# Two fused VectorE instructions per tile for the feed-forward norms of layer 2, and an earlier place for GpSimd's clearing of a table

## The chip, the cores and the metric

The kernel runs on one core of a Trainium2 chip, as one program with one launch. The metric is the device time of that program in microseconds. Its engines are TensorE (PE; PEld is its weight load), VectorE (DVE), ScalarE (ACT), GpSimd (POOL) and SyncE (SP, which only issues DMAs). Each works through its own queue in order and waits on semaphores where it needs another's result, or its own earlier one.

## The reference, cut to what matters

Four layers of attention, cross-attention and feed-forward, each added to x (4 sequences of 256 tokens, 128 wide). Changed is work of layer 2's feed-forward, which holds two normalisations with weight and bias:

```python
x = x + _L2_ffn_ref(_layernorm(x, axis=-1), ln1_w, ln1_b, w1, b1, ln2_w, ln2_b, w2, b2)

def _L2_ffn_ref(x, ln1_w, ln1_b, w1, b1, ln2_w, ln2_b, w2, b2):
    def layernorm(x, w, b):
        mu = jnp.mean(x, axis=-1, keepdims=True)
        var = jnp.mean(jnp.square(x - mu), axis=-1, keepdims=True)
        return (x - mu) * jax.lax.rsqrt(var + EPS) * w + b
    ...
    h = layernorm(x, ln1_w, ln1_b)          # 128 wide
    h = bitlinear(h, w1, b1)                # activations to 8 bits, weights to -1, 0, 1; 128 -> 512
    h = jax.nn.gelu(h, approximate=False)
    h = layernorm(h, ln2_w, ln2_b)          # 512 wide
    out = bitlinear(h, w2, b2)              # 512 -> 128
    return out
```

## The kernel before, in words

Tokens lie on the 128 partitions: a batch (one sequence of 256 tokens) is two tiles of 128 tokens. The program is a row of stages. Around the change two of them run into each other: `stacked_attention`, which does the attentions of layer 2 (its last batches run here), and `feedforward_attentions`, which does layer 2's feed-forward and both attentions of layer 3. Each is written out in steps, with one list for each engine of what it issues in a step. `overlapped` puts the two lists of an engine together: step s of the second stage comes behind step s + 176 (`SHIFT`) of the first. So the place of an instruction in an engine's queue is fixed by its step, and no scheduler moves it.

In the first stage each step has a score product of one head (lines 650 and 651) into one of three PSUM banks, whose maximum VectorE takes (L847) and so frees the bank; a second score product (L661, L662) behind which ScalarE takes the exponential (L831); and in groups the product with the values (L755). After a batch's 16 heads VectorE splits the maxima in bf16 parts (L852 to L858) and TensorE transposes them (L698). L866 normalises values, L702 and L714 are the output's transposes and products.

In the second stage `PLAN` gives for each piece of the feed-forward the step for each of the four batches. "in" takes the statistics of x, "twice" normalises x into XN (two L2378) and takes the statistics of that, "norm1" normalises again and applies weight and bias, "quant1" rounds to 8 bits (L2387 to L2402), f1 transposes (L2153, copied by L2519), f2 multiplies by w1 (L2157, scaled by L2523 into H), "gelu" is ScalarE's, "hidden" takes the statistics of H (512 wide), "norm2" and "affine2" normalise it and apply weight and bias, "quant2" rounds, f3 transposes (L2163, copied by L2521) and f4 multiplies by w2 (L2168, added to x by L2526 to L2530). After that the attention of layer 3 begins: L2173 transposes the normalised x, L2179 makes queries and keys, L2242 scores, L2544 their maxima.

Statistics go to `moments` (mean and variance by tile). GpSimd makes rstd from them, `deviation`: a tensor_scalar that adds eps (L2591) and a power (L2593), behind which the semaphore rstd is raised. The function `centred` waits for that and issues for each tile one tensor_scalar with two columns as scalars, mean and rstd (L2378). `own` counts an instruction and `own.settle()` waits until all counted ones are through, so an instruction between two settles can't overlap with its neighbours; the two of a pair can.

```python
PLAN = {"in": (-58, -42, -24, -9), "twice": (-54, -38, -20, -6), "norm1": (-50, -34, -16, -2), "quant1": (-49, -33, -11, -1),
        ...
        "affine2": (-23, -11, 5, 15), ...}
FROM, TO = PLAN["in"][0], jobs[-1][0] + 1
```

MTR is a table of the row maxima's bf16 parts (4096 bf16 columns, in `space`) that layer 3's second score product reads; most of its rows stay zero, so GpSimd clears it once, with `bout` behind it. The readers are SyncE's copies into it and the job "b" (L2517).

Of the kernel before, what the change touches and what calls it, by code (L numbers as in the profile page):

```python
# [11 lines left out]
ALU = mybir.AluOpType  # L12
# [3 lines left out]
B, L, D = 4, 256, 128  # L16
# [23 lines left out]
                   ln2w=(128, 512), ln2b=(128, 512)),  # L40
# [150 lines left out]
def bcast(ap, at, n):  # L191

    a = ap.unsqueeze(at)
    shape = list(a.shape)
    shape[at] = n
    return a.broadcast_to(shape)
# [1759 lines left out]
def feedforward_attentions(c, before, shift):  # L1956


    nc, PS, s = c.nc, c.PS, c.space
    n = "l23"  # L1960
    WF, WA, WX = c.W["l2_ffn"], c.W["l3_attn"], c.W["l3_xattn"]
# [33 lines left out]
    stats, moments = over(TILES * 6).rearrange("p (t i) -> p t i", t=TILES), over(TILES * 2).rearrange("p (t i) -> p t i", t=TILES)  # L1995
# [10 lines left out]
    var, rstd = ({x: sem("_%s_%s" % (y, x)) for x in ("in", "twice", "hidden", "attn", "cross", "out")} for y in ("var", "rstd"))  # L2006
# [357 lines left out]
    def vector(dve, own):  # L2364
# [10 lines left out]
        def centred(kind, b, src, dst, mom, index, done=None):  # L2375
            dve.wait_ge(rstd[kind], b + 1)
            for t in range(2):
                ins = nc.vector.tensor_scalar(dst(t), src(t), mom[:, index + t, 0:1], c.rstd[:, index + t:index + t + 1],  # L2378
                                              ALU.subtract, ALU.mult)
                if done is None:  # L2380
                    own(ins)
                else:
                    ins.then_inc(done, 1)

        def quantise(b, h, tmp, q, weight, done):
            li, st, iv = (a[:, b % 2, weight, :] for a in (lim, step_, inv))
            own(nc.vector.tensor_reduce(li, h, AX_X, ALU.max, apply_absolute_value=True))  # L2387
            own.settle()
            own(nc.vector.tensor_scalar(li, li, 1e-5, None, ALU.max))
            own.settle()  # L2390
            own(nc.vector.reciprocal(st, li))
            if (b, weight) != (0, 0):
                own(nc.vector.tensor_scalar(iv, li, 1.0 / 127, wmean[:, weight:weight + 1], ALU.mult, ALU.mult))
            own.settle()
            own(nc.vector.tensor_scalar(st, st, 127.0, None, ALU.mult))
            own.settle()
            for t in range(2):
                own(nc.vector.tensor_scalar(tmp[:, t, :], h[:, t, :], st[:, t:t + 1], 127.0, ALU.mult, ALU.min))
            own.settle()
            own(nc.vector.tensor_scalar(tmp, tmp, -128.0, MAGIC, ALU.max, ALU.add))  # L2400
            own.settle()
            nc.vector.tensor_scalar(q, tmp, MAGIC, None, ALU.subtract).then_inc(done, 1)  # L2402
# [3 lines left out]
        def feedforward(what, b):  # L2406
            h = H[:, b % 2]
            ht, hn = (lambda t: h[:, t, :]), (lambda t: h[:, t, 0:D])
            if what == "in":
                statistics("in", b, xt(b), c.stats, c.moments, tile(b))  # L2410
            elif what == "twice":
                centred("in", b, xt(b), xnt(b), c.moments, tile(b))
                statistics("twice", b, xnt(b), stats, moments, tile(b))
            elif what == "norm1":
                centred("twice", b, xnt(b), hn, moments, tile(b))
                own.settle()
                own(nc.vector.tensor_tensor(h[:, :, 0:D], h[:, :, 0:D], bcast(WF["ln1w"], 1, 2), ALU.mult))
                own.settle()
                own(nc.vector.tensor_tensor(h[:, :, 0:D], h[:, :, 0:D], bcast(WF["ln1b"], 1, 2), ALU.add))
                own.settle()  # L2420
            elif what == "quant1":
                if b >= 2:
                    dve.wait_ge(*emptied("f3", b - 2, 0))
                quantise(b, h[:, :, 0:D], T[:, :, 0:D], Q[:, b % 2, :, 0:D], 0, q_ready)
            elif what == "hidden":
                dve.wait_ge(gelu_done, 2 * b + 2)
                statistics("hidden", b, ht, stats, moments, tile(b))
            elif what == "norm2":
                centred("hidden", b, ht, ht, moments, tile(b))
                own.settle()  # L2430
                own(nc.vector.tensor_tensor(h, h, bcast(WF["ln2w"], 1, 2), ALU.mult))
                own.settle()
            elif what == "affine2":
                own(nc.vector.tensor_tensor(h, h, bcast(WF["ln2b"], 1, 2), ALU.add))
                own.settle()
            elif what == "quant2":
                quantise(b, h, T, Q[:, b % 2], 1, q2_ready)
            elif what == "attn":
                statistics("attn", b, xt(b), c.stats, c.moments, tile(b))
            elif what == "normed":  # L2440
                centred("attn", b, xt(b), xnt(b), c.moments, tile(b), xn_ready)
            else:
                own.settle()
                own(nc.vector.reciprocal(wscale, wmean))
                own(nc.vector.tensor_scalar(inv[:, 0, 0, :], lim[:, 0, 0, :], 1.0 / 127, wmean[:, 0:1], ALU.mult, ALU.mult))
                own.settle()
                for i, w in enumerate(("w1", "w2")):
                    own(nc.vector.tensor_scalar(T[:, i, :], WF[w], wscale[:, i:i + 1], 1.0, ALU.mult, ALU.min))
                own.settle()
                own(nc.vector.tensor_scalar(T, T, -1.0, MAGIC, ALU.max, ALU.add))  # L2450
                own.settle()
                for i in range(2):
                    nc.vector.tensor_scalar(WQ[:, i, :], T[:, i, :], MAGIC, None, ALU.subtract).then_inc(weights_ready, 1)
# [133 lines left out]
    def gpsimd(pool, own):  # L2587
# [38 lines left out]
        for step in range(FROM, TO):  # L2626
            yield step
            for what, b in pieces(step, "in", "twice", "hidden", "attn", "cross", "out"):
                deviation(what, b, moments if what in ("twice", "hidden") else c.moments)
            if step == FROM + 14:  # L2630
                nc.gpsimd.memset(MTR, 0.0).then_inc(fills, 1)
                nc.gpsimd.memset(bout, 0.0).then_inc(fills, 1)
            if step == -2:
                pool.wait_ge(before.pv_done, before.units // 4)
                pool.wait_ge(*before.q_saved)
                pool.wait_ge(*before.k_saved)
                nc.gpsimd.memset(VB[:, :, :, :, WIDE:WIDE + 1], 1.0).then_inc(fills, 1)
            for p in pieces(step, "products", "shift", "values", "scale"):
                if p[1] not in SHARED or p[0] != "shift":
                    cross(*p)  # L2640
# [333 lines left out]
```

## Time and profile before

| | |
|---|---|
| Median of 3 runs | 1099.58 us (1098.29 to 1102.47) |
| The profiled execution | 1095.55 us |
| its span | 1093.7 us |
| TensorE busy | 815.3 us (75%) |
| VectorE busy | 611.6 us (56%) |
| ScalarE busy | 349.3 us (32%) |
| GpSimd busy | 316.2 us (29%) |

The span is the time from the first to the last recorded instruction, and the execution's own time has what lies around it. Times in the profile count from the start of the span. A busy share is a mean over stages with different limits, so it says little of the stage in question. In a timeline's row the number in brackets is idle time of the engine ahead of the row, with what ended it. In the rows of groups, 128x512 is partitions by elements.

### The profile page before, as it was taken

What the parts mean: (1) busy time and instruction counts of PE and PEld (TensorE: products, weight loads), DVE (VectorE), ACT (ScalarE), POOL (GpSimd) and SP (SyncE); (2) the same over time, 40 slices, a digit from 0 to 9 for tenths busy, and PEclk for the clock granted to TensorE, in tenths of its full rate; (3) what the DMA queues carried; (4) which work ended last, traced back from release to release, by engine and by line L of the source; (5) the groups of instructions that cost most, each with busy time, mean ns of one, the idle gap of its engine ahead of it and who ended that gap; (6) DMA issues with size and microseconds to landing.
All of it is one profiled execution on the core that took longest, in us unless ns stands there. A gap on an engine that the chain in (4) does not pass through costs nothing. (4 is left out here: it accounts for less than half of the span.)

```text
span 1093.7 us, 15967 instructions
## 1 busy us (share of the span) xinstructions
PE 815.3 (75%) x5969; PEld 591.4 (54%) x5969; DVE 611.6 (56%) x1414; ACT 349.3 (32%) x683; POOL 316.2 (29%) x318
## 2 busy tenths in 40 slices
PE   4974797892686275688877755999999996167994
PEld 2542453581353164567645433677777686144994
DVE  2654872323669962886666787764345545843222
ACT  1110474331121111245535541444342332011331
POOL 1354200203238723332221211000053433415232
PEclk9985798896688676999989886999999998558897
DMA  9302200361000003544473000000000000005685
GB/s 370 148 2 86 70 7 1 93 189 36 20 1 1 0 1 73 111 92 85 112 203 88 3 1 1 2 1 2 1 2 1 2 1 1 0 1 184 211 285 161
DMA packets 44678, 72.44 MB, mean 66 GB/s; under 512 B 4817, under 2 KB 36737, under 8 KB 43033
## 3 DMA queue, kind: packets, MB, share of 16 engines
q1 hardware_dynamic: 38921, 65.72, 20.4%
q0 software_dynamic: 1728, 3.59, 1.0%
q10 hardware_dynamic: 3952, 2.10, 0.7%
q8 instruction: 48, 0.79, 0.3%
q14 instruction: 29, 0.24, 0.1%
HBM read 58.65 MB, written 15.89 MB: 68 GB/s over the span
## 5 line engine op out<-in xcount | busy, mean ns | idle before, releaser
L847 DVE TENSOR_REDUCE space<-PS 128x2 f32<-128x512 f32 x128 | 83.2, 686 | 40.1 <-PE PS L651 39.7
L2544 DVE TENSOR_REDUCE space<-PS 128x2 f32<-128x512 f32 x64 | 43.3, 689 | 83.0 <-PE PS L2242 82.8
L831 ACT ACTIVATE annex<-PS 128x384 f32<-128x384 f32 (+1 forms) x128 | 67.2, 544 | 57.9 <-PE PS L662 29.2
L2279 PEld LDWEIGHTS PS<-space 128*128 128x128 f32 x512 | 61.2, 191 | 16.8 <-issue 16.5
L2279 PE MATMUL PS<-space 128*128 128x65 f32 x512 | 68.6, 280 | 0.0
L2259 PE MATMUL PS<-space 64*128 64x256 f32 x256 | 67.1, 403 | 0.2 <-ACT space L2362 0.2
L1947 POOL TENSOR_TENSOR space<-space 128x1536 f32<-128x1536 f32 x16 | 54.6, 3435 | 32.7 <-ACT space L1820 26.4
L2242 PE MATMUL PS<-space 64*128 64x256 f32 x256 | 62.7, 401 | 0.1
L1170 PE MATMUL PS<-space 128*128 128x128 f32 x444 | 58.2, 287 | 4.2 <-ACT space L1239 2.3
L1305 DVE TENSOR_TENSOR space<-PS,space 128x512 f32<-128x512 f32 (+1 forms) x28 | 19.2, 687 | 74.3 <-ACT space L1232 69.2
L1170 PEld LDWEIGHTS PS<-space 128*128 128x128 f32 x444 | 54.4, 200 | 6.8 <-issue 3.8
L2591 POOL TENSOR_SCALAR var_eps<-moments 128x2 f32<-128x2 f32 x16 | 3.5, 220 | 188.1 <-DVE moments L2373 188.1
L2362 ACT ACTIVATE space<-PS 128x512 f32<-128x512 f32 x64 | 37.1, 596 | 56.3 <-PE PS L2260 56.2
L2242 PEld LDWEIGHTS PS<-space 64*128 64x128 f32 x256 | 37.8, 186 | 20.5 <-issue 14.1
L226 PE MATMUL PS<-small_tile 128*128 128x512 bf16 x40 | 17.6, 619 | 32.2 <-DVE moments L211 31.5
L831 ACT ACTIVATE space<-PS 128x512 f32<-128x512 f32 x64 | 35.7, 599 | 11.8 <-PE PS L662 10.7
L1340 POOL DMA_INDIRECT l_ffn_y<-space x22 | 21.1, 957 | 54.9 <-ACT space L1223 54.9
L2179 PE MATMUL PS<-XT,weights 128*128 128x256 f32 x128 | 34.9, 410 | 1.2 <-DVE const_tile L2519 0.7
L2606 POOL TENSOR_TENSOR weights<-CTX,annex 128x2048 f32<-128x2048 f32 x6 | 26.9, 4500 | 30.2 <-ACT CTX L2340 18.6
L2617 POOL TENSOR_TENSOR weights<-const_tile,annex 128x2048 f32<-128x2048 f32 x6 | 32.6, 5442 | 7.4 <-ACT const_tile L2354 7.4
L1789 PE MATMUL PS<-const_tile,annex 128*128 128x128 f32 x64 | 14.8, 318 | 26.4 <-DVE annex L1934 26.4
L2259 PEld LDWEIGHTS PS<-space 64*128 64x128 f32 x256 | 32.3, 186 | 2.7 <-issue 0.5
(492 smaller groups left out, 2196.3 us busy)
## 6 DMA issues: line engine op xcount, KB each, us to landing
space<-in_e_l_ffn SPq DMA_DIRECT2D x22, 768.0 KB, 4.6
space<-in_e_l_ffn SPq DMA_DIRECT2D x23, 192.0 KB, 3.0
l_ffn_sorted<-in_slots SPq DMA_DIRECT2D x2, 1584.0 KB, 25.6
space<-l_attn_scratch_k SPq DMA_DIRECT2D x8, 384.0 KB
space<-l_ffn_sorted SPq DMA_DIRECT2D x10, 264.0 KB, 4.2
weights<-in_w_l_xattn SPq DMA_DIRECT2D x1, 2504.0 KB, 15.2
weights<-in_w_l_attn SPq DMA_DIRECT2D x1, 2124.0 KB, 12.0
space<-l_xattn_scratch_q SPq DMA_DIRECT2D x4, 512.0 KB, 3.4
```

Of the source, the lines that this page charges most:

```text
L831: nc.scalar.activation(P[:, u % 8, 0:keys], PS[:, 3 + u % 2, 0:keys], ACT.Exp).then_inc(exp_done, 1)
L847: nc.vector.tensor_reduce(m[:, :, at_h], max_bank(u).rearrange("p (c k) -> p c k", c=2), AX_X, ALU.max).then_inc(max_done, 1)
L1170: last = nc.tensor.matmul(PS[:, 2 * kind + g % 2, 128 * i:128 * i + 128], weight(b, kind, chunk), x, start=True, stop=True)
L1947: nc.gpsimd.tensor_tensor(PR[:, j - 1, :, :], Q[:, t % 2, :, :], bcast(KG[:, t, j, :], 1, 16), ALU.mult).then_inc(prod, 1)
L2179: last = nc.tensor.matmul(out[:, 256 * (g % 2):256 * (g % 2) + 256], w[:, 128 * g:128 * g + 128], c.XT[:, sl], start=True, stop=True)
L2242: last = nc.tensor.matmul(PS[:, max_bank[a], 256 * qc:256 * qc + 256], q[:, 128 * qc:128 * qc + 128], kk, start=True, stop=True)
L2259: nc.tensor.matmul(out, kk[:, 128 * kc:128 * kc + 128], q, start=True, stop=False)
L2279: last = nc.tensor.matmul(out, p[:, 256 * kc + 128 * qc:256 * kc + 128 * qc + 128], VB[:, b % 2, kc, h, :], start=kc == 0, stop=kc == 1)
L2362: nc.scalar.activation(P[i % 4], PS[:, exp_bank[i], :], ACT.Exp).then_inc(exp_done, 1)
L2544: nc.vector.tensor_reduce(MX[:, b % 2, :, h], PS[:, max_bank[a], :].rearrange("p (c k) -> p c k", c=2), AX_X, ALU.max).then_inc(max_done, 1)
L2606: nc.gpsimd.tensor_tensor(PR[:, t, :].rearrange("p (h g d) -> p h g d", h=16, g=16), bcast(heads(QX, t), 2, 16), bcast(heads(KX, t), 1, 16 ...
L2617: nc.gpsimd.tensor_tensor(PR[:, t, :].rearrange("p (h d g) -> p h d g", h=16, d=8), bcast(e[:, t, :].rearrange("p (h g) -> p h g", h=16), ...
```

## The change

Two things. First, `centred` and two tensor_tensor (weight, bias) give way to two scalar_tensor_tensor for each tile: `weighted` takes (x - mean) * weight, `shifted_by` takes that times rstd, plus bias. In norm1 both follow one another; of layer 2's second norm `weighted` stands in norm2 and `shifted_by` in affine2. The wait for rstd moves from the first instruction to the second. Second, the clearing of MTR and bout is issued in step FROM + 2 = -56 instead of FROM + 14 = -44.

```diff
@@ -2382,6 +2382,18 @@
                 else:
                     ins.then_inc(done, 1)
 
+        def weighted(kind, b, src, dst, weight):
+            dve.wait_ge(var[kind], 2 * b + 2)
+            for t in range(2):
+                own(nc.vector.scalar_tensor_tensor(dst(t), src(t), moments[:, tile(b) + t, 0:1], weight, ALU.subtract, ALU.mult))
+            own.settle()
+
+        def shifted_by(kind, b, h, bias):
+            dve.wait_ge(rstd[kind], b + 1)
+            for t in range(2):
+                own(nc.vector.scalar_tensor_tensor(h(t), h(t), c.rstd[:, tile(b) + t:tile(b) + t + 1], bias, ALU.mult, ALU.add))
+            own.settle()
+
         def quantise(b, h, tmp, q, weight, done):
             li, st, iv = (a[:, b % 2, weight, :] for a in (lim, step_, inv))
             own(nc.vector.tensor_reduce(li, h, AX_X, ALU.max, apply_absolute_value=True))
@@ -2412,12 +2424,8 @@
                 centred("in", b, xt(b), xnt(b), c.moments, tile(b))
                 statistics("twice", b, xnt(b), stats, moments, tile(b))
             elif what == "norm1":
-                centred("twice", b, xnt(b), hn, moments, tile(b))
-                own.settle()
-                own(nc.vector.tensor_tensor(h[:, :, 0:D], h[:, :, 0:D], bcast(WF["ln1w"], 1, 2), ALU.mult))
-                own.settle()
-                own(nc.vector.tensor_tensor(h[:, :, 0:D], h[:, :, 0:D], bcast(WF["ln1b"], 1, 2), ALU.add))
-                own.settle()
+                weighted("twice", b, xnt(b), hn, WF["ln1w"])
+                shifted_by("twice", b, hn, WF["ln1b"])
             elif what == "quant1":
                 if b >= 2:
                     dve.wait_ge(*emptied("f3", b - 2, 0))
@@ -2426,13 +2434,9 @@
                 dve.wait_ge(gelu_done, 2 * b + 2)
                 statistics("hidden", b, ht, stats, moments, tile(b))
             elif what == "norm2":
-                centred("hidden", b, ht, ht, moments, tile(b))
-                own.settle()
-                own(nc.vector.tensor_tensor(h, h, bcast(WF["ln2w"], 1, 2), ALU.mult))
-                own.settle()
+                weighted("hidden", b, ht, ht, WF["ln2w"])
             elif what == "affine2":
-                own(nc.vector.tensor_tensor(h, h, bcast(WF["ln2b"], 1, 2), ALU.add))
-                own.settle()
+                shifted_by("hidden", b, ht, WF["ln2b"])
             elif what == "quant2":
                 quantise(b, h, T, Q[:, b % 2], 1, q2_ready)
             elif what == "attn":
@@ -2627,7 +2631,7 @@
             yield step
             for what, b in pieces(step, "in", "twice", "hidden", "attn", "cross", "out"):
                 deviation(what, b, moments if what in ("twice", "hidden") else c.moments)
-            if step == FROM + 14:
+            if step == FROM + 2:
                 nc.gpsimd.memset(MTR, 0.0).then_inc(fills, 1)
                 nc.gpsimd.memset(bout, 0.0).then_inc(fills, 1)
             if step == -2:
```

VectorE's queue at norm1 of batch 0, before: the two tensor_scalar of "twice", its statistics, four maxima, norm1, a maximum and the head of quant1 (`weights` is where H, T and moments lie).

```order
L2378 TENSOR_SCALAR XN<-X,moments,rstd 128x128 x2
L2370 BN_STATS weights<-XN 128x6 x2
L2373 BN_AGGR weights<-weights 128x2 x2
L847 TENSOR_REDUCE space<-PS 128x2 x4
L2378 TENSOR_SCALAR weights<-XN,weights,rstd 128x128 x2
L2417 TENSOR_TENSOR weights<-weights 128x2x128
L2419 TENSOR_TENSOR weights<-weights 128x2x128
L847 TENSOR_REDUCE space<-PS 128x2
L2387 TENSOR_REDUCE weights<-weights 128x2
```

The same place in the changed kernel:

```order
L2378 TENSOR_SCALAR XN<-X,moments,rstd 128x128 x2
L2370 BN_STATS weights<-XN 128x6 x2
L2373 BN_AGGR weights<-weights 128x2 x2
L847 TENSOR_REDUCE space<-PS 128x2 x4
L2388 SCALAR_TENSOR_TENSOR weights<-XN,weights 128x128 x2
L2394 SCALAR_TENSOR_TENSOR weights<-weights,rstd 128x128 x2
L847 TENSOR_REDUCE space<-PS 128x2
L2399 TENSOR_REDUCE weights<-weights 128x2
```

Four instructions in place of four, all of one tile each now, and nothing around them has moved (L2399 is L2387 under its new number).

VectorE's queue at norm2 and affine2 of batch 0, before:

```order
L2519 COPY const_tile<-PS 128x256
L2378 TENSOR_SCALAR weights<-weights,rstd 128x512 x2
L2431 TENSOR_TENSOR weights<-weights 128x1024
L2370 BN_STATS stats<-X 128x6 x2
L2373 BN_AGGR moments<-stats 128x2 x2
L864 RECIPROCAL space<-PS 128x16
L866 TENSOR_TENSOR annex<-PS,space 128x2x64
L2523 SCALAR_TENSOR_TENSOR weights<-PS,weights 128x512 x2
L2434 TENSOR_TENSOR weights<-weights 128x1024
```

and in the changed kernel:

```order
L2523 COPY const_tile<-PS 128x256
L2388 SCALAR_TENSOR_TENSOR weights<-weights 128x512 x2
L2370 BN_STATS stats<-X 128x6 x2
L2373 BN_AGGR moments<-stats 128x2 x2
L864 RECIPROCAL space<-PS 128x16
L866 TENSOR_TENSOR annex<-PS,space 128x2x64
L2527 SCALAR_TENSOR_TENSOR weights<-PS,weights 128x512 x2
L2394 SCALAR_TENSOR_TENSOR weights<-weights,rstd 128x512 x2
```

Three instructions became two at norm2, and one became two at affine2; the line numbers of the copy and of f2's scaling are four higher.

GpSimd's queue where the second stage begins, before:

```order
L2591 TENSOR_SCALAR var_eps<-moments 128x2
L2593 TENSOR_TENSOR rstd<-var_eps,neghalf 128x2
L2591 TENSOR_SCALAR var_eps<-weights 128x2
L2593 TENSOR_TENSOR rstd<-var_eps,neghalf 128x2
L2631 MEMSET space 128x4096
L2632 MEMSET space 128x128
L2591 TENSOR_SCALAR var_eps<-moments 128x2
```

and in the changed kernel:

```order
L2595 TENSOR_SCALAR var_eps<-moments 128x2
L2597 TENSOR_TENSOR rstd<-var_eps,neghalf 128x2
L2635 MEMSET space 128x4096
L2636 MEMSET space 128x128
L2595 TENSOR_SCALAR var_eps<-weights 128x2
L2597 TENSOR_TENSOR rstd<-var_eps,neghalf 128x2
L2595 TENSOR_SCALAR var_eps<-moments 128x2
```

The two memsets have moved past one deviation, that of "twice" of batch 0, and now stand between it and that of "in".

## Rows read from the trace of the kernel before

**Rows 1.** TensorE's waits from 600 to 680 us (us in total, times, longest)

```profile
PE PS L2163 <- DVE const_tile L2519: 5.9, 1, 5.9
PE PS L2153 <- DVE const_tile L2402: 5.1, 1, 5.1
PE PS L702 <- DVE annex L866: 4.3, 1, 4.3
```

**Rows 2.** Busy us in stretches: length, PE, PEld, DVE, ACT, POOL, clock

```profile
609.00:615.00 6.00, 2.96 (x14) 1.62 (x12) 5.30 (x18) 2.05 (x4) 0.00 (x0) 0.50 0.00 0
615.00:619.00 4.00, 4.00 (x26) 2.37 (x24) 0.00 (x0) 0.96 (x2) 0.00 (x0) 0.56 0.03 6
640.00:671.00 31.00, 9.91 (x76) 6.69 (x74) 27.44 (x80) 4.47 (x7) 4.73 (x11) 0.65 0.00 0
...
680.00:740.00 60.00, 57.83 (x354) 40.67 (x355) 42.67 (x91) 28.87 (x57) 3.73 (x8) 1.00 0.01 1
```

**Rows 3.** GpSimd's timeline (start us, us, engine, line)

```profile
597.80 0.71 POOL L2593 TENSOR_TENSOR rstd<-var_eps,neghalf 128x2 f32<-128x2 f32 x1
...
603.36 3.51 POOL L2631 MEMSET space<- 128x4096 bf16 x1
...
651.27 0.71 POOL L2593 TENSOR_TENSOR rstd<-var_eps,neghalf 128x2 f32<-128x2 f32 x1
```

**Rows 4.** VectorE's timeline around the clearing, 600 to 608 us

```profile
600.90 0.59 DVE L2378 TENSOR_SCALAR XN<-X,moments,rstd 128x128 f32<-128x128 f32 x2
...
602.22 2.45 DVE L847 TENSOR_REDUCE space<-PS 128x2 f32<-128x512 f32 x4
604.59 2.58 DVE L2378 TENSOR_SCALAR weights<-XN,weights,rstd 128x128 f32<-128x128 f32 x2
```

**Rows 5.** TensorE's timeline, 598 to 618 us

```profile
598.54 0.28 PE L661 MATMUL PS<-space 114*128 114x256 bf16 x1 [0.84 <-ACT annex L831]
...
605.38 1.07 PE L755 MATMUL PS<-annex,space 128*32 128x256 f32 x16
608.87 0.40 PE L650 MATMUL PS<-space 114*128 114x256 bf16 x1 [2.41 <-DVE space L847]
...
614.83 0.38 PE L698 MATMUL PS<-small_tile,space 128*48 128x128 bf16 x2 [1.37 <-DVE space L858]
...
617.57 1.52 PE L755 MATMUL PS<-annex,space 128*32 128x256 f32 x16
```

**Rows 6.** VectorE's groups by form, 590 to 745 us (busy us, mean ns)

```profile
L2523 DVE SCALAR_TENSOR_TENSOR weights<-PS,weights 128x512 f32<-128x512 f32 x8 | 5.8, 742 | 3.3 <-PE PS L2157 3.3
...
L2431 DVE TENSOR_TENSOR weights<-weights 128x1024 f32<-128x1024 f32 x4 | 4.9, 1226 | 0.1
...
L890 DVE TENSOR_TENSOR X<-PS,X 128x256 f32<-128x256 f32 x4 | 1.7, 421 | 2.5 <-PE PS L714 2.5
...
L2528 DVE SCALAR_TENSOR_TENSOR X<-PS,weights,X 128x128 f32<-128x128 f32 x3 | 1.1, 351 | 0.1
```

**Rows 7.** VectorE's timeline, 627 to 658 us

```profile
627.25 0.60 DVE L2378 TENSOR_SCALAR weights<-XN,weights,rstd 128x128 f32<-128x128 f32 x2
...
628.80 0.42 DVE L2387 TENSOR_REDUCE weights<-weights 128x2 f32<-128x256 f32 x1
...
635.55 0.43 DVE L890 TENSOR_TENSOR X<-PS,X 128x256 f32<-128x256 f32 x1 [2.46 <-PE PS L714]
...
637.53 0.99 DVE L2378 TENSOR_SCALAR weights<-weights,rstd 128x512 f32<-128x512 f32 x2
...
641.03 1.40 DVE L2523 SCALAR_TENSOR_TENSOR weights<-PS,weights 128x512 f32<-128x512 f32 x2
642.34 1.22 DVE L2434 TENSOR_TENSOR weights<-weights 128x1024 f32<-128x1024 f32 x1
...
651.40 0.43 DVE L2417 TENSOR_TENSOR weights<-weights 128x256 f32<-128x256 f32 x1
...
657.27 0.42 DVE L2526 TENSOR_TENSOR X<-X,weights 128x256 f32<-128x256 f32 x1 [1.60 <-PE PS L2168]
```

## The prediction

> **What bounds the kernel now.** I read the busy shares of the page, then the clock and busy time by stretch, then who waits for whom in the stretch that holds the changed work, and last the timelines of VectorE, GpSimd and TensorE there. The changed work lies between 597 and 740 us of a span of 1093.7. From 680 us on TensorE has no slack: 57.83 us busy of 60 between 680 and 740, at full clock, with VectorE at 42.67 [rows 2]. Whatever VectorE saves there is hidden. Before 680 it is the other way round. Between 640 and 671 TensorE is busy for 9.91 us of 31 and VectorE for 27.44 [rows 2], and TensorE's longest waits there are all for VectorE: 5.9 us for the copy of L2519, 5.1 for the quantised rows of L2402, 4.3 for the normalised values of L866 [rows 1]. None of these three is itself a changed instruction, but each stands in VectorE's queue behind changed ones. The same holds between 605 and 615: TensorE idles 2.41 us until a maximum (L847) frees its bank, and 1.37 us until the last of L858 is there [rows 5]. So a microsecond taken from VectorE counts in these two stretches if nothing between it and 680 us waits for another engine.
>
> **The clearing of MTR.** It is one 3.51 us memset (3511 ns) on GpSimd at 603.36 [rows 3], with one of 128 columns behind it. Beside it VectorE's two L2378 of norm1 for batch 0 take 2.58 us [rows 4], where the same pair takes 0.60 us at 627.25 [rows 7]: 1.98 us lost, and the pair ends at 604.59 + 2.58 = 607.17, 0.30 us after the memset's end at 606.87. The row shows one instruction held until the other engine is through, while the four maxima between 602.22 and 604.59 ran beside the same memset at their usual 0.6 us each [rows 4].
> The Trainium skill ("SBUF — State Buffer", section "SBUF: two separate sides") says that the port pair which VectorE and GpSimd share is an exclusive lock, held for a whole instruction against a VectorE operation in a two-port mode; by that rule, the trace agrees, the loser waits to the end of the memset.
>
> Twelve steps sooner does not mean twelve steps of time. GpSimd's queue is in order and holds nothing between: the clearing now stands behind the first pair of L2591 and L2593. That one ends at 597.80 + 0.71 = 598.51 [rows 3], so the memset runs from about 598.47 to 601.98. At 600.90 VectorE comes to the two L2378 of "twice" for batch 0, the same kind of instruction [rows 4]. They will be held: end at 601.98 + 0.30 = 602.28 instead of 600.90 + 0.59 = 601.49. So the move trades a stall of 1.98 us for one of 0.79. Queued behind the held pair are the statistics of "twice", then the four maxima, whose banks TensorE needs. The next GpSimd step (deviation of "twice", var_eps for batch 0) needs those statistics at about 603.1, and GpSimd is free by then, so nothing waits for the clearing itself. Bounds of the stall: 0, if the memset is over by 600.90, and 1.1, if the whole pair starts only behind it (601.98 + 0.60 - 601.49).
>
> **The price of a fused instruction.** No scalar_tensor_tensor with two inputs in SBUF and a column as scalar is in the trace. Nearest: L2528, 128x128, 351 ns, and L2523, 128x512, 742 ns, both with PSUM as one input; a pair of L2523 takes 1.40 us [rows 6, 7]. That PSUM makes no difference is seen on plain tensor_tensor of 128x256: 421 ns with it (L890), 0.43 us without (L2417) [rows 6, 7]. So I take 0.35 and 0.75 us, and for pairs 0.61 and 1.40. A lower bound is a pair of the plain tensor_tensor that has the same elements, 1.226 us [rows 6]; an upper one two instructions with no overlap, 1.50.
> norm1: now 0.60 + 0.43 + 0.42 and gaps, 627.25 to 628.80 = 1.55 us [rows 7]; then two pairs, 2 x 0.61 + 2 x 0.04 = 1.30. Saves 0.25.
> norm2: now 0.99 + 0.04 + 1.23 = 2.26 [rows 6, 7]; then one pair and a gap, 1.43. Saves 0.83.
> affine2: now 1.22 + 0.04 = 1.26 [rows 7]; then 1.43. Costs 0.17.
> Together 0.91 us for a batch, 3.6 us of VectorE's time for four. The affine step gets dearer: the old tensor_tensor did both tiles at once and needed no scalar. The first fused instruction no longer waits for rstd; the second does, a step later for norm2. No wait of norm1 or norm2 for rstd is in the trace, so this gains nothing.
> A rule of the skill speaks against the new form. "SBUF — State Buffer", the same section, has a VectorE operation with two SBUF inputs contend with a GpSimd operation that reads SBUF. The row: the two-input L2417 at 651.40 lies inside GpSimd's power at 651.27 to 651.98, and neither is longer than its kind (0.43 and 0.71 us) [rows 3, 7]. By the row the fused ones lose nothing. By the rule each could wait up to one power, 0.71 us, where they meet; the old tensor_tensor had the same exposure.
>
> **What reaches the end.** Stretch 1, to 614.8: VectorE works up to the last of L858 with hardly a gap (5.30 us of the 6 from 609 on), and TensorE waits for it at 608.87 and 614.83 [rows 2, 5]. Gain: 1.98 - 0.79 + 0.25 = 1.44 us. TensorE is then busy without a gap until 619 [rows 2], and the chain goes on from there, shifted.
> Batch 1's norm1 at 627.25 is followed by a wait of VectorE's for TensorE (2.46 us until 635.55, which is behind the gelu and the exponentials of ScalarE), so its 0.25 is hidden [rows 7].
> Stretch 2, 637.53 to 671: norm2 of batch 0 brings L2523 at 641.03 earlier, not by 0.83 but by about 0.75, since TensorE's product must be there. Then affine2 (0.17 lost) and norm1 of batch 2 (0.25 won) stand ahead of L866: 0.83 earlier. norm2 of batch 1 comes after L866, and behind it VectorE waits 1.60 us for TensorE at 657.27 [rows 7]: its 0.83 is hidden, and only its affine2 costs, 0.17. Net 0.75 - 0.17 + 0.25 - 0.17 = 0.66.
> Batch 3's norm1 lies in VectorE's next wait for TensorE, and norm2 and affine2 of batches 2 and 3 (from 695) lie beside a full TensorE [rows 2]: nothing.
> Sum: 1.44 + 0.66 = 2.1 us. The profiled execution took 1095.55 us; 1095.55 - 2.1 = 1093.45. It lies 4.0 us below the median of the runs, 1099.58, which gives 1099.58 - 2.1 = 1097.5 us, or 0.2%. A change under about 0.5% (5.5 us) can't be told from none here: the three runs of the kernel before lie 4.2 us apart.
>
> **Rivals.**
> A, the sum above: 1097.5. Chance 0.62. With the bounds of the prices (stall 0 to 1.1; pairs of 1.23 to 1.50): the gain is 2.1 - 0.3 - 3 x 0.1 = 1.5 at the least and 2.1 + 0.8 + 3 x 0.17 = 3.4 at the most, 1096.2 to 1098.1.
> B, TensorE keeps its full clock after 609. It fell to 0.50 in 609 to 615 and 0.56 in 615 to 619, after the idle of 2.41 us [rows 2, 5]. With that idle cut to about 1 us it may stay up. A group of 16 of L755 takes 1.07 us at 605.38 and 1.52 at 617.57 [rows 5], so the 4.2 us between 614.83 and 619 would shrink to about 2.5 to 2.9: 1.5 us more, 1096.0. Against it: between 607 and 613 TensorE still gets only four short groups. 0.15.
> C, the other side: the stall now falls where TensorE is full (600 to 606). If the short idle that it makes there brings the clock down at 603 instead of 609, the 3.4 us of TensorE's work up to 606.45 take up to twice as long (1.52 / 1.07 for L755, more for short ones); with 3.0 us lost, VectorE waits for scores and the result is 2.1 - 3.0 = 0.9 us slower, 1100.5. It decides once TensorE loses more than 2.1 us. Against it: the idle would be 0.8 us at most, and at 598.54 an idle of 0.84 us is followed by work at the old pace [rows 5]. 0.10.
> D, hidden anyway: the gain of stretch 1 or 2 is taken up by ScalarE's exponentials or by GpSimd's rstd, which stand between the two stretches. Left: 1 us or less, 1098.6 to 1099.6. 0.10. The last 0.03 is for something that I don't see.
>
> **How the numbers follow.** Likeliest A, 1097.5. Faster by over 0.5% needs 5.5 us: B, and as much again from the clock later on, or luck of the runs: 0.17. Slower by over 0.5%: C with a second fall of the clock, or the same luck: 0.06. Within: 0.77. The cases span 1096.0 to 1100.5; the spread of the runs (2.9 us above, 1.3 below their median) belongs on top: 1093.0 to 1101.5.
>
> **What the profile of the changed kernel would show.** GpSimd's memset at about 598.5, one of the two L2378 near 600.9 at some 1.1 us or more, and none of the L2388 near 605 over 0.4. Fused instructions of 0.35 and 0.74 us. The first maximum (L847) behind norm1 at about 606.7, TensorE's idle before L650 cut from 2.41 to about 1; f4's addition for batch 0 (L2526, now at 657.27) about 2.3 us earlier; everything from 680 on 2.1 us earlier, in stretches of unchanged length. Wrong would make it: fused instructions of 0.9 us or more at 128x512, a clock that falls elsewhere than at 609, or a VectorE that no longer bounds 640 to 671.

## The result: slightly slower, 1104.88 us against 1099.81

The changed kernel has a median of 1104.88 us in 20 runs (1098.29 to 1111.54), the kernel before 1099.81 us in 20 (1094.81 to 1104.79). The ratio is 1.0048 with a 95% interval of 1.0028 to 1.0068: about 5 us slower, where the prediction had 2 us faster. A second measurement of the same pair (below) gives 1.0031 [1.0007, 1.0055]. So the sign is settled, the size is between 1 and 7 us.

The profiled execution took 1109.24 us, with a span of 1107.4. Its page shows the engines nearly as before: VectorE has 4.6 us less to do (611.6 before), TensorE is 10 us longer busy (815.3) with as many instructions to run.

```profile
PE 825.3 (75%) x5969; PEld 599.3 (54%) x5969; DVE 607.0 (55%) x1414; ACT 348.9 (32%) x683; POOL 316.5 (29%) x318
```

More busy time for the same products means a lower clock somewhere. But the two profiled executions are 13.7 us apart, and the change isn't all of that. To see where the time went I took four marks that both timelines have: the bias scaling of L2570 (L2574 in the changed kernel), which stands just ahead of the changed work; L2188, TensorE's transposes of the last batch's row maxima in layer 3, the longest of its waits for VectorE between 740 and 870 us (the others there are 1.17 us or less); the first L208, the statistics with which the last stage begins; and the end of the span. Timelines of the changed kernel, VectorE at the first and third mark, TensorE at the second:

```profile
602.58 0.16 DVE L2574 TENSOR_SCALAR space<-weights 128x8 f32<-128x8 f32 x1
869.77 0.27 PE L2188 MATMUL PS<-small_tile,space 128*48 128x128 bf16 x2 [1.47 <-DVE space L2560]
974.36 1.65 DVE L208 BATCH_NORM_STATS2 stats<-X 128x6 f32<-128x128 f32 x8 [1.88 <-PEq L2864]
```

and of the kernel before:

```profile
596.57 0.16 DVE L2570 TENSOR_SCALAR space<-weights 128x8 f32<-128x8 f32 x1
864.68 0.27 PE L2188 MATMUL PS<-small_tile,space 128*48 128x128 bf16 x2 [1.50 <-DVE space L2556]
966.20 1.65 DVE L208 BATCH_NORM_STATS2 stats<-X 128x6 f32<-128x128 f32 x8 [1.86 <-PEq L2860]
```

| | before | changed | difference |
|---|---|---|---|
| start to the scaling | 596.57 | 602.58 | +6.0 |
| scaling to L2188 | 268.11 | 267.19 | -0.9 |
| L2188 to L208 | 101.52 | 104.59 | +3.1 |
| L208 to the end of the span | 127.5 | 133.0 | +5.5 |

The first and the last row hold no changed instruction, and they scatter by nearly as much in the kernels below, whatever is changed in them (starts of 597.01 to 602.65, ends of 127.7 to 132.3). The instructions ahead of the scaling are the same in all but the last of them. The two in the middle come back from profile to profile: 268.1 and 268.4, then 101.5 and 101.6 for two profiles of the kernel before; 267.2 and 267.0, then 104.6 and 104.6 for two of the changed one. So the changed work does save time, though 0.9 to 1.4 us instead of 2.1, and then 3.1 us are lost in a stretch that the change doesn't touch.

**The changed instructions** are as forecast. VectorE's timeline, changed kernel:

```profile
606.91 1.36 DVE L2378 TENSOR_SCALAR XN<-X,moments,rstd 128x128 f32<-128x128 f32 x2
...
611.37 0.60 DVE L2388 SCALAR_TENSOR_TENSOR weights<-XN,weights 128x128 f32<-128x128 f32 x2
612.00 0.61 DVE L2394 SCALAR_TENSOR_TENSOR weights<-weights,rstd 128x128 f32<-128x128 f32 x2
...
619.02 0.19 DVE L858 TENSOR_TENSOR space<-space 128x32 bf16<-128x32 f32 x1
624.40 0.29 DVE L2523 COPY const_tile<-PS 128x256 bf16<-128x256 bf16 x1 [5.19 <-PE PS L2153]
...
643.01 0.29 DVE L2523 COPY const_tile<-PS 128x256 bf16<-128x256 bf16 x1 [1.77 <-PE PS L2153]
643.22 1.41 DVE L2388 SCALAR_TENSOR_TENSOR weights<-weights 128x512 f32<-128x512 f32 x2
...
662.17 0.43 DVE L2530 TENSOR_TENSOR X<-X,weights 128x256 f32<-128x256 f32 x1 [2.45 <-PE PS L2168]
```

GpSimd's timeline shows the clearing beside which that first pair of L2378 is held:

```profile
604.48 3.51 POOL L2635 MEMSET space<- 128x4096 bf16 x1
```

and VectorE's groups by form, 596 to 750 us (busy us, mean ns):

```profile
L2394 DVE SCALAR_TENSOR_TENSOR weights<-weights,rstd 128x512 f32<-128x512 f32 x8 | 5.6, 746 | 0.0
L2388 DVE SCALAR_TENSOR_TENSOR weights<-weights 128x512 f32<-128x512 f32 x8 | 5.6, 744 | 0.0
...
L2394 DVE SCALAR_TENSOR_TENSOR weights<-weights,rstd 128x128 f32<-128x128 f32 x8 | 2.5, 348 | 0.1
L2388 DVE SCALAR_TENSOR_TENSOR weights<-XN,weights 128x128 f32<-128x128 f32 x8 | 2.4, 340 | 0.0
```

**The lost 3.1 us** show in the clock by stretch. The columns are those of [rows 2], and the figure behind POOL's count is the granted clock. The changed kernel:

```profile
863.00:870.00 7.00, 5.53 (x42) 3.80 (x38) 3.97 (x10) 2.14 (x4) 5.92 (x2) 1.00 0.01 2
870.00:877.00 7.00, 7.00 (x37) 4.98 (x36) 5.25 (x4) 2.13 (x5) 1.06 (x1) 0.54 0.02 4
877.00:880.00 3.00, 3.00 (x27) 2.46 (x26) 0.61 (x2) 0.92 (x2) 2.00 (x1) 0.94 0.00 0
```

The kernel before, in which L2188 starts 5.1 us earlier:

```profile
858.00:865.00 7.00, 5.50 (x42) 3.77 (x38) 4.08 (x10) 2.03 (x5) 5.83 (x2) 1.00 0.01 2
865.00:882.00 17.00, 16.78 (x148) 13.90 (x150) 10.22 (x15) 7.49 (x14) 10.98 (x3) 1.00 0.01 2
```

Ahead of L2188 the two are alike, the wait is alike too (1.47 and 1.50 us), and behind it TensorE is full in both. But in the changed kernel the clock is at 0.54 for 7 us, near the lower of its two levels (1.2 GHz), and TensorE gets through 37 matmuls; in the kernel before it stays at the upper one (2.4 GHz), with 148 matmuls in 17 us. TensorE's timeline right behind the wait, changed kernel: the second group of four L2259 takes 1.08 us, and the same group before, at 865.53, 0.60.

```profile
869.97 0.71 PE L2259 MATMUL PS<-space 64*128 64x256 f32 x4
870.51 0.38 PE L2260 MATMUL PS<-space,small_tile 64*128 64x256 bf16 x2
870.67 1.08 PE L2259 MATMUL PS<-space 64*128 64x256 f32 x4
```

### The profile page after: what moved, and what is told of

Its sections match the earlier page's. It is cut to its first block and busy times, and to the rows that moved or that the text cites. A ratio compares the mean times of both kernels' runs of the same rounds, so it can differ in the third digit from the quotient of the medians.

```text
span 1107.4 us, 15972 instructions
## 1 busy us (share of the span) xinstructions
PE 825.3 (75%) x5969; PEld 599.3 (54%) x5969; DVE 607.0 (55%) x1414; ACT 348.9 (32%) x683; POOL 316.5 (29%) x318
## 5 line engine op out<-in xcount | busy, mean ns | idle before, releaser
L847 DVE TENSOR_REDUCE space<-PS 128x2 f32<-128x512 f32 x128 | 83.4, 685 | 40.2 <-PE PS L651 39.9
L2259 PE MATMUL PS<-space 64*128 64x256 f32 x256 | 68.6, 415 | 0.0
L1170 PE MATMUL PS<-space 128*128 128x128 f32 x444 | 55.5, 278 | 8.1 <-DVE space L1305 5.5
L2242 PEld LDWEIGHTS PS<-space 64*128 64x128 f32 x256 | 37.8, 186 | 20.4 <-issue 13.7
L755 PE MATMUL PS<-annex,space 128*32 128x256 f32 (+1 forms) x512 | 34.6, 391 | 0.0
```

What stands on the lines that cost most here:

```text
L755: last = nc.tensor.matmul(out, VA[:, b, v:v + 32], moving, start=kc == 0, stop=kc == 1, tile_position=(0, row))
L847: nc.vector.tensor_reduce(m[:, :, at_h], max_bank(u).rearrange("p (c k) -> p c k", c=2), AX_X, ALU.max).then_inc(max_done, 1)
L1170: last = nc.tensor.matmul(PS[:, 2 * kind + g % 2, 128 * i:128 * i + 128], weight(b, kind, chunk), x, start=True, stop=True)
L2242: last = nc.tensor.matmul(PS[:, max_bank[a], 256 * qc:256 * qc + 256], q[:, 128 * qc:128 * qc + 128], kk, start=True, stop=True)
L2259: nc.tensor.matmul(out, kk[:, 128 * kc:128 * kc + 128], q, start=True, stop=False)
```

## Experiments

The theory after this profile: this wait of about 1.5 us is in every version; whether TensorE's clock falls behind it depends on when it comes, and the change moved it by about 1 us. The rivals: that one of the two parts costs time by itself (another layout of the fused norms, the new place of the clearing), or that the slowdown is chance.

The ratios are against the kernel before, run on the same chip. In the table at the end of this section are the marks of all profiles.

### Each part alone

**The kernel before and the changed one, measured again.** No edit.

> The kernel before again, unchanged, as a control. All theories expect a ratio of 1.000 within 0.002. Its profile shows how far two executions of one program differ before 597 us, in the changed stretch and in the tail: theory A (the changed stretch is faster by about 0.7 us, the loss lies in stages that don't hold the change) expects 3 to 6 us of scatter outside the changed stretch and under 1 us in it.

> The changed kernel again. 1.003 to 1.007 if the loss is a property of the program, 1.000 if it was one of the runs. Theory A: from the first deviation of the second stage (L2595) to the first L2242 the profile takes some 0.7 us less than before, as in the first profile, and the loss is behind it or ahead of it.

Measured: 0.9983 [0.9962, 1.0004] for the control (the same program on both sides), 1.0031 [1.0007, 1.0055] for the changed kernel, medians 1098.60 and 1103.37 us. The clock in 870 to 877 us of the second is 0.53 again. So the slowdown isn't chance. The control also shows how little a ratio can tell: one and the same program differs from itself by 0.17%.

**The fused norms alone**, with the clearing in its old place:

```diff
-            if step == FROM + 2:
+            if step == FROM + 14:
```

> Fused norms alone; the clearing stays in step FROM + 14. If the norms carry the loss: 1.003 to 1.007. If the place of the clearing carries it: 0.998 to 1.000. By the prediction's own sum 0.25 + 0.66 = 0.9 us faster, and the first L2388 pair beside the memset is not held (0.6 us and not 2.6), so that the stall of 1.98 us would go too and this version would beat the changed one by 0.8 us.

**The clearing alone**, with the old norms:

```diff
-            if step == FROM + 14:
+            if step == FROM + 2:
```

> The earlier clearing alone, old norms. If the place of the clearing carries the loss: 1.003 to 1.007. If the norms do: 0.998 to 1.000; by the sum 1.2 us faster, with one L2378 pair at 1.4 us near 601 and norm1 of batch 0 at 1.55 us.

The norms alone: 1.0103 [1.0065, 1.0141], 1110.55 us, over twice as bad as the whole change, where 0.8 us less than the changed kernel had been expected. The clearing alone: 1.0009 [0.9983, 1.0034], 1101.89 us, no difference. Clock by stretch, norms alone:

```profile
867.00:884.00 17.00, 16.97 (x84) 13.28 (x86) 7.66 (x10) 4.14 (x8) 10.06 (x3) 0.53 0.01 1
```

and the clearing alone:

```profile
866.00:873.00 7.00, 7.00 (x49) 5.24 (x49) 5.91 (x6) 2.89 (x6) 1.06 (x1) 0.76 0.02 4
```

Both have the fall behind L2188 (which starts at 867.03 and 865.97), one for all of 17 us, the other for some 3 of 7. The parts don't add up: +11 us and +1 us make +3 to +5. That speaks against a price of either part and for the moment of the wait. But by these four alone the norms could still be the cause, through their layout or something that I don't see.

### The wait filled, and the old timing restored with the new norms

**Fill.** Six matmuls of 512 bf16 columns, whose result nobody reads, into the bank that L2188 is going to write, ahead of its wait. They are useless work, added to three kernels: the changed one, the one before, and the fused norms alone.

```diff
             elif kind == "M":
+                if b == B - 1:
+                    for _ in range(6):
+                        nc.tensor.matmul(out, c.identb, c.small_tile[:, 0:512], start=True, stop=True)
                 pe.wait_ge(max_parts, b + 1)
```

> The changed kernel, with six useless matmuls (512 columns, bf16) put into TensorE's queue ahead of its wait for the last batch's maxima (L2188, idle 1.47 us), into the bank that L2188 overwrites. Theory A (the shifted arrival of this idle brings the clock down behind it, 2.85 us lost in both profiles of the changed kernel): the clock stays at 1.00 behind L2188, and the ratio falls from about 1.004 to 0.998 to 1.001. Theory B (the fused instructions or the program's layout cost time elsewhere): nothing changes, 1.003 to 1.005.

> The kernel before with the same six matmuls. Its two profiles show no fall of the clock behind L2188. Theory A: 0.998 to 1.000, no more than the falls that some executions may have. Theory B: 1.000.

> Fused norms alone with the same six matmuls. Theory A: its profile lost 7.65 us behind L2188 with the clock at 0.50, so the ratio falls from 1.010 to 1.000 to 1.003. Theory B: it stays at 1.009 to 1.011.

**Pad.** The fused norms alone, with useless VectorE work that gives the time saved back: one instruction of 128x64 behind norm1 and one of 128x1024 behind norm2, in each batch.

```diff
                 shifted_by("twice", b, hn, WF["ln1b"])
+                own(nc.vector.tensor_scalar(T[:, 0, 0:64], T[:, 0, 0:64], 1.0, None, ALU.mult))
+                own.settle()
...
                 weighted("hidden", b, ht, ht, WF["ln2w"])
+                own(nc.vector.tensor_scalar(T, T, 1.0, None, ALU.mult))
+                own.settle()
```

> Fused norms alone, with useless VectorE instructions that give back what they save: a tensor_scalar of 128x64 behind norm1 (some 0.25 us with its gap) and one of 128x1024 behind norm2's (some 0.73). Theory A: everything arrives when it did before, the clock stays up behind L2188, and the version with more work is faster than the one without by 6 to 9 us: 0.999 to 1.002. Theory B: 1.010 or a little more.

Measured: the changed kernel filled 0.9984 [0.9953, 1.0016], 1099.83 us; the kernel before filled 0.9986 [0.9967, 1.0005], 1098.96; the norms filled 1.0012 [0.9989, 1.0035], 1100.90; the norms padded 1.0005 [0.9979, 1.0030], 1100.19. So the same six matmuls take about 1% off the norms alone and nothing that can be told off the kernel before, and padding, which only adds work, makes the norms alone about 1% faster. The fused instructions stand in both where they stood. TensorE's timeline, norms filled (the trace has five of the six matmuls; the real transposes are L2191 there, and the fill doesn't delay them: they come 266.9 us behind the scaling, and 267.0 without it):

```profile
862.51 1.24 PE L2188 MATMUL PS<-small_tile 128*128 128x512 bf16 x5
863.87 0.29 PE L2191 MATMUL PS<-small_tile,space 128*48 128x128 bf16 x2
```

and the clock by stretch behind it:

```profile
864.00:881.00 17.00, 16.78 (x147) 13.80 (x147) 10.29 (x15) 7.30 (x14) 10.71 (x3) 1.00 0.01 2
```

147 matmuls in 17 us, where the norms alone got 84. The padding came out larger than meant: in batch 0 its 128x64 instruction, a tensor_scalar, runs beside the clearing and takes 1.19 us, in the other batches 0.20. So the wait comes 0.5 to 0.8 us later than in the kernel before, and not when it did there. The norms padded have L2188 at 869.25 with the wait in it, and no fall:

```profile
869.00:886.00 17.00, 16.52 (x144) 13.71 (x146) 10.19 (x17) 6.93 (x14) 10.41 (x3) 1.00 0.01 2
```

### The same fall without any of the change, and the best version

**Late.** The kernel before, with its old norms and the clearing in its old place, and behind norm2 of batch 0 one or three useless VectorE instructions of 128x1024. The last of the three kernels has the three and the fill.

```diff
                 own(nc.vector.tensor_tensor(h, h, bcast(WF["ln2w"], 1, 2), ALU.mult))
                 own.settle()
+                for _ in range(3 if b == 0 else 0):
+                    own(nc.vector.tensor_scalar(T, T, 1.0, None, ALU.mult))
+                    own.settle()
```

> The kernel before, old norms, with one useless VectorE instruction (128x1024, 0.73 us) behind norm2 of batch 0 alone, on the path: L2188 comes about 0.7 us later. Theory A (only the moment at which TensorE's idle before L2188 comes decides on the clock) allows a fall or none; the padded norms stood 0.8 us later than before and had none, so 1.000 to 1.001. A theory that each shift does harm: 1.003 or more.

> The kernel before with three such instructions, L2188 about 2.2 us later; no fused instruction and the old place of the clearing. Theory A: with old norms too some shift must bring the clock down; this one is my guess for it: the profile shows 0.50 behind L2188 for 3 us or more, and the time is 2.2 us for the delay plus 3 to 8 for the fall, 1.004 to 1.009. Theory B (the fall belongs to the fused norms): no fall, 2.2 us, 1.002.

> The last one with the six matmuls in TensorE's idle before L2188. Theory A: the delay alone is left, 1.001 to 1.003, below the last one by 3 to 8 us, at a granted clock of 1.00 behind L2188. Theory B: as the last one.

**Clearing first, filled.** The changed kernel with the fill, and the two memsets ahead of step FROM's deviation, so that they run far from the first pair of L2378.

```diff
             yield step
+            if step == FROM:
+                nc.gpsimd.memset(MTR, 0.0).then_inc(fills, 1)
+                nc.gpsimd.memset(bout, 0.0).then_inc(fills, 1)
...
-            if step == FROM + 2:
-                nc.gpsimd.memset(MTR, 0.0).then_inc(fills, 1)
-                nc.gpsimd.memset(bout, 0.0).then_inc(fills, 1)
```

> The changed kernel with the six matmuls and with the clearing ahead of the deviation of in (step FROM), where GpSimd idles for 15.8 us. The pair L2378 near 600 is then not held (0.60 us, not 1.36): 0.8 us less before L2188 than the changed kernel, 267.1 to about 266.3 from the bias scaling to L2188. The fastest of the versions by the sum: 2.9 us under before, 0.9965 to 0.9985, if the clock falls nowhere else.

One late instruction: 0.9998 [0.9977, 1.0019], 1101.53 us. Three: 1.0088 [1.0054, 1.0121], 1110.80 us, and filled 1.0021 [0.9994, 1.0047], 1103.24 us. The three move L2188 by 2.2 us (270.6 against 268.4), and what they cost beyond that is gone with the fill. TensorE's timeline with the three late ones, and its clock by stretch:

```profile
871.53 0.27 PE L2188 MATMUL PS<-small_tile,space 128*48 128x128 bf16 x2 [1.49 <-DVE space L2559]
```

```profile
871.00:888.00 17.00, 16.47 (x80) 13.05 (x82) 8.10 (x13) 4.14 (x8) 9.22 (x3) 0.54 0.01 1
888.00:896.00 8.00, 8.00 (x40) 5.92 (x38) 0.61 (x2) 1.08 (x2) 2.64 (x1) 0.50 0.01 2
```

This is the changed kernel's loss, and a larger one, in a kernel that has neither a fused norm nor a moved memset. So a shift of what stands ahead of the wait makes it, in both directions: with the wait 0.3 to 1 us earlier and 2.2 us later than in the kernel before.

The clearing first and filled: 0.9978 [0.9957, 0.9999], 1097.83 us. That is the lowest ratio of all, and well below the changed kernel's; from the kernel before it can't be told, whose own control came out at 0.9983. VectorE's timeline shows that its first pair of L2378 (here L2381) is no longer held:

```profile
602.14 0.60 DVE L2381 TENSOR_SCALAR XN<-X,moments,rstd 128x128 f32<-128x128 f32 x2
```

Most of the 0.76 us that this saves doesn't arrive: scaling to L2188 takes 266.9 us, where the changed kernel filled takes 267.1 and I had expected 266.3. The last of L858 does come 0.77 us sooner behind the scaling (15.69 us against 16.46), but the interval between VectorE's two copies of f1 behind it takes 19.10 us against 18.60, with the clock at 0.51 from 630 to 636 us.

Marks of the profiles, us (for filled kernels the second mark is the real transpose, L2191), and the ratio. The column in the middle ends where TensorE next waits for long, 2.6 us at L2194 (L2197 in filled kernels):

| kernel | scaling to L2188 | L2188 to L2194 | L2188 to L208 | ratio |
|---|---|---|---|---|
| before | 268.1, 268.4 | 48.4, 48.4 | 101.5, 101.6 | 0.9983 |
| changed | 267.2, 267.0 | 51.3, 51.3 | 104.6, 104.6 | 1.0048, 1.0031 |
| norms alone | 267.0 | 56.1 | 109.5 | 1.0103 |
| clearing alone | 267.9 | 49.7 | 101.9 | 1.0009 |
| changed, filled | 267.1 | 48.4 | 102.0 | 0.9984 |
| before, filled | 268.3 | 48.4 | 101.6 | 0.9986 |
| norms, filled | 266.9 | 48.4 | 102.0 | 1.0012 |
| norms, padded | 268.9 | 48.4 | 100.8 | 1.0005 |
| before, 1 late | 268.7 | 48.4 | 101.2 | 0.9998 |
| before, 3 late | 270.6 | 59.3 | 112.6 | 1.0088 |
| before, 3 late, filled | 270.6 | 48.4 | 102.0 | 1.0021 |
| clearing first, filled | 266.9 | 48.4 | 102.0 | 0.9978 |

Of the kernels whose wait isn't filled, those with 268.1 to 268.9 us from the scaling to L2188 keep the clock, and those with 267.0 to 267.9 or 270.6 lose it. Without a fall L2188 to L2194 takes 48.4 us in every profile, filled or not, so this column gives the price of the fall alone: 1.3, 2.9, 7.7 and 10.9 us.

The rest, L2194 to L208, isn't constant either (52.3 to 53.6 us), for the same thing happens at L2194 on a smaller scale: in the kernel before the clock is at 0.50 from 914 to 918 us. TensorE's timelines, the kernel before, and the clearing alone, which wins back 0.9 us there:

```profile
913.07 1.94 PE L2194 MATMUL PS<-const_tile,annex 128*128 128x128 f32 x8 [2.60 <-DVE annex L2564]
```

```profile
915.63 1.06 PE L2194 MATMUL PS<-const_tile,annex 128*128 128x128 f32 x8 [2.59 <-DVE annex L2564]
```

## Why the prediction was wrong, step by step

**The step that failed** is the last of "What the profile would show": "everything from 680 on 2.1 us earlier, in stretches of unchanged length". The sum had ended at 680 us, because TensorE is full behind that [rows 2]. I took it that a stretch that is only shifted keeps its length. It doesn't: 190 us later TensorE waits 1.47 us for VectorE's maxima (L2188), as before, and this time the clock falls behind it. 3.1 us lost there in the profiles, against 0.9 won, gives +2.2 us. Shown: the wait is needed for the loss (the fill removes it in three kernels), and neither the fused norms nor the clearing's place is (three late old instructions bring it about, and padding removes it with the fused norms in place). What decides is how the work ahead of the wait is shifted, at an unchanged length of the wait. The measured 1104.88 us also lies above the prediction's range of 1093.0 to 1101.5. That range isn't what its words give: cases from 1096.0 to 1100.5 with 1.3 us below and 2.9 above are 1094.7 to 1103.4, which still ends too low. A clock that falls elsewhere than at 609 was the prediction's own sign of being wrong. The mechanism was that of rival C, a short idle of TensorE that brings its clock down, at another place: I had looked for it only where the change makes a new idle, and not at the idles that it merely moves.

**The clearing** cost what was forecast, to 0.02 us: a stall of 0.77 us, forecast 0.79. The pair at 606.91 takes 1.36 us, forecast 1.38 (602.28 - 600.90), with the memset's end at 604.48 + 3.51 = 607.99 and the pair's 0.28 behind it. But the 1.98 us that the prediction credited to the move would have come without it: with the norms alone, whose clearing is in the old place, nothing is held (see the last section).

**The fused instructions**: 348 and 340 ns at 128x128, forecast 350; 746 and 744 at 128x512, forecast 750; pairs 0.60, 0.61 and 1.41, forecast 0.61 and 1.40. The last of L858 comes, counted from the scaling, after 619.02 - 602.58 = 16.44 us, where it took 614.49 - 596.57 = 17.92: 1.48 us won in stretch 1, forecast 1.44. The sum of the two changes was right there, its split wasn't: to the same point the clearing alone wins 1.23 us (forecast 1.19) and the norms alone 2.26 (forecast 0.25), and together they win less than the norms alone.

**Between the two stretches** the prediction's "the chain goes on from there, shifted" failed as well, and this is where 2.1 became 0.9. From L858 to f1's copy (L2519 before, L2523 now) TensorE works alone. That took 619.35 - 614.49 = 4.86 us and takes 624.40 - 619.02 = 5.38 now: 0.52 lost. (The second pair of profiles has 5.06 and 5.38, 0.32 lost.) TensorE's timeline and clock by stretch, changed kernel:

```profile
609.71 0.28 PE L650 MATMUL PS<-space 114*128 114x256 bf16 x1 [0.63 <-DVE space L847]
...
613.40 0.28 PE L650 MATMUL PS<-space 114*128 114x256 bf16 x1 [0.17 <-DVE space L847]
...
616.11 0.28 PE L650 MATMUL PS<-space 114*128 114x256 bf16 x1 [2.09 <-DVE space L847]
...
619.36 0.38 PE L698 MATMUL PS<-small_tile,space 128*48 128x128 bf16 x2 [2.05 <-DVE space L858]
...
622.10 1.94 PE L755 MATMUL PS<-annex,space 128*32 128x256 f32 x16
```

```profile
615.00:619.00 4.00, 1.21 (x8) 0.68 (x8) 3.81 (x11) 1.36 (x3) 0.00 (x0) 0.87 0.00 0
619.00:624.00 5.00, 4.64 (x27) 2.57 (x28) 0.19 (x1) 0.96 (x2) 0.00 (x0) 0.50 0.02 5
```

and of the kernel before, the second of its two waits for L847, which [rows 5] leaves out:

```profile
611.57 0.40 PE L650 MATMUL PS<-space 114*128 114x256 bf16 x1 [1.67 <-DVE space L847]
```

The clock still falls, but later against the work: before, it was down from 609 and nearly up again by 619, so the group of L755 took 1.52 us [rows 2, 5]; now it is up through the short groups, the whole group of L755 runs at 0.50, and it takes 1.94. So rival B came half true, and to the other effect: the fall behind 609 is gone, the next one costs more. The wait of 2.41 us for L847 [rows 5], forecast at 1 us, is the one at 613.40 now (each is the first L650 behind a group of L755): 0.17. VectorE is 1.48 us sooner and TensorE 0.78 later, partly because the held pair makes it wait 0.63 us at 609.71, with the clock at 1.00 behind it. The next wait for L847 grew from 1.67 to 2.09 and the one for L858 from 1.37 to 2.05, since TensorE, now at full clock, is through with its short groups sooner. The next interval, copy to copy, took 637.32 - 619.35 = 17.97 us and takes 643.01 - 624.40 = 18.61: 0.64 lost (0.43 in the second pair of profiles). Its L755 group at 641.13 takes 1.40 us, and 1.07 before. Rival D had a loss between the stretches, but by ScalarE or GpSimd; here the first loss, and the larger part of the second, stand beside TensorE's low clock.

**Stretch 2**: copy to f4's addition took 657.27 - 637.32 = 19.95 us [rows 7] and takes 662.17 - 643.01 = 19.16. 0.79 won, forecast 0.83; 0.17 more was forecast to be lost behind it, which gave the 0.66. So 1.48 - 0.52 - 0.64 + 0.79 = 1.1 us by f4's addition, and 0.9 by L2188.

**What stays open.** The profiles account for +2.2 us (+1.7 in the second pair), the ratios for 3.4 and 5.3, and the changed kernel's runs spread wider (13 us against 10). That in other executions the fall is longer than in these two (the profiles of other kernels have it from about 3 to 24 us long) would fit, and the fill takes all of it off, but I have no profile of the changed kernel in which it is. Nor is it shown why just these moments bring the clock down, and no run moved the wait by itself: each shift also moved TensorE's earlier waits against one another, and most kernels have a single profile. Absolute time isn't it: the two profiles of the kernel before start L2188 at 864.68 and 868.32 without a fall, the norms alone at 867.03 with one. The interval to the scaling, 267 to 271 us, goes with it, but both profiles of one kernel share everything else too.

## What to carry to other kernels

Where TensorE is nearly full but for a wait of a microsecond or two, a shift of 1 to 2 us ahead of it can cost 1 to 11 us behind it, or nothing; so read the granted clock behind every wait that the change shifts, not only behind those that it makes. When two variants differ by more than their parts explain, fill that wait with useless matmuls in both, and compare again: what is left (here 0.9984 for the changed kernel and 0.9986 for the one before, no difference that runs can show) is the worth of the edit. A saving on VectorE has to be followed through every interval in which TensorE sets the pace at its lower clock, since of 2.1 us 1.2 were lost in two such intervals before anything else went wrong.

## What the runs showed of the hardware

One and the same wait of 1.47 to 1.50 us, with TensorE full behind it, was followed by no change of the clock in the kernel before, the one with one late instruction and the padded one, but by about 3 us at 0.50 with the clearing alone, 7 us with the whole change, 17 us with the norms alone and some 24 us with three late instructions. TensorE had work all that time. A wait of 1.17 us at 768.18 in the kernel before (L2194) was followed by no fall in any of them. Two neighbouring waits show the same: the group of eight L2194 behind an idle of 2.6 us took 1.94 us in the kernel before, 1.27 in the changed one and 1.06 with the clearing alone.

A fused instruction with two inputs in SBUF isn't held by a memset, while a tensor_scalar is. With the norms alone the old place of the clearing puts it beside norm1. VectorE's and GpSimd's timelines there:

```profile
608.04 0.60 DVE L2388 SCALAR_TENSOR_TENSOR weights<-XN,weights 128x128 f32<-128x128 f32 x2
```

```profile
606.82 3.51 POOL L2635 MEMSET space<- 128x4096 bf16 x1
```

The memset runs to 610.33, and both pairs (the second at 608.68, 0.61 us) go through at their usual length, where the old pair of L2378 in that place took 2.58 us [rows 4]. In the padded kernel, the useless tensor_scalar of 128x64 behind them runs beside the same memset and takes 1.19 us instead of 0.20:

```profile
609.66 1.19 DVE L2429 TENSOR_SCALAR weights<-weights 128x64 f32<-128x64 f32 x1
```

So with the fused norms the clearing needn't have moved: its new place makes a stall of 0.76 us that its old one no longer has, though at L2188 no more than 0.2 us of it are left (267.0 us against 267.2 and 267.0). The Trainium skill ("SBUF — State Buffer", section "SBUF: two separate sides") has a VectorE operation with two SBUF inputs contend only with a GpSimd operation that reads SBUF, and a memset reads nothing; by that rule, the trace agrees.
